# Expert gates in two halves, a reordered lead-in and earlier gathers in a two-layer metaformer kernel

## The reference, cut to what matters

```python
# layer 0 mixer, per image: depthwise 3x3 value and query; stride-2 key and offsets
o = gelu(ln(off) * ln_g + ln_b)                 # 28 x 28 points
offset = tanh(einsum(o, w_off2) + ref_points)   # sampling positions
sampled = bilinear(value, offset)               # 4 neighbours, gathered
x = x + w_out @ (query @ (key, sampled))        # linear attention
# both layers, per pixel t: mixture of experts
probs = softmax(ln(t) @ gate_w + gate_b)        # 4 experts
masked = probs * top2(probs); masked /= masked.sum() + 1e-9
t = t + sum_e masked[e] * (gelu(ln(t) @ w1[e] + b1[e]) @ w2[e] + b2[e])
# layer 1 mixer: sum of 7x7, 5x3, 3x5 and separable depthwise convolutions
```

## Time and profile before

| | |
|---|---|
| median of 3 runs | 1770.33 us (1766.41 to 1772.63) |
| the profiled execution: its time, its span | 1774.66 us, 1772.7 us |
| PE busy | 1429.3 us, 81% |
| DVE busy | 962.2 us, 54% |
| ACT busy | 681.6 us, 38% |
| POOL busy | 283.9 us, 16% |
| first matmul of slot 0 | at 300.4 us |
| steps 1 to 6 of slot 7 (nothing beside the experts) | 16.94 us each |

### The profile page before, as it was taken

One profiled execution on the slowest core, in us unless ns is written; L12 is line 12 of the kernel. 1 busy time (PEld: TensorE's weight loads), 2 busy tenths in 40 slices (PEclk: granted clock), 3 DMA queues, 4 the chain that ended last, 5 costly groups with the idle time before them and its releaser, 6 DMA issues.

```text
span 1772.7 us, 19232 instructions
## 1 busy us (share of the span) xinstructions
PE 1429.3 (81%) x6068; PEld 959.2 (54%) x6068; DVE 962.2 (54%) x2534; ACT 681.6 (38%) x1403; POOL 283.9 (16%) x189
## 2 busy tenths in 40 slices
PE   4120635888876999898976999899989999999898
PEld 2110324555544567665644567666766676666565
DVE  3968864747897454346887454444343443244323
ACT  3120023424543333344543334345344434355443
POOL 2514021701126000001117000000000000000000
PEclk9999955898997999999888999999999999999999
DMA  3441120413332322223323322234223412221121
GB/s 104 90 107 57 39 66 20 134 60 97 94 99 79 102 64 72 66 80 98 107 66 93 103 75 72 66 96 109 61 63 82 124 52 57 67 78 44 56 69 44
DMA packets 169510, 137.94 MB, mean 78 GB/s; under 512 B 114752, under 2 KB 163138, under 8 KB 169026
## 3 DMA queue, kind: packets, MB, share of 16 engines
q1 hardware_dynamic: 162802, 131.26, 27.2%
q0 software_dynamic: 3072, 4.82, 1.0%
q10 hardware_dynamic: 3536, 0.63, 0.2%
HBM read 97.02 MB, written 39.65 MB: 77 GB/s over the span
## 4 chain that ended last, share of the span: by engine, by line
issue 42%; PE 38%; POOL 10%; ACT 4%; DVE 3%; DMA 1%; ACTq 1%; SPq 1%; POOLq 0%; DVEq 0%
PE y_ps L898 15%; PE at_ps L1001 7%; POOL ln_rstd L811 5%; POOL pix_mem L824 5%; PE h_ps L906 4%; PE h_ps L907 4%; PE h_ps L905 4%; ACT ln_cen L679 2%; PE lg_ps L888 1%; PE lb_ps L879 1%; PE at_ps L954 1%; ACT hidden L772 1%; ACTq L655 1%; DVE vq_mem L1174 1%; DVE part L1130 0%
## 5 line engine op out<-in xcount | busy, mean ns | idle before, releaser
L772 ACT ACTIVATE hidden<-h_ps,b 128x448 f32<-128x448 f32 x672 | 425.0, 634 | 750.8 <-PE h_ps L907 746.6
L898 PE MATMUL y_ps<-hidden,w 128*96 128x448 f32 x1344 | 639.6, 560 | 44.6 <-ACT hidden L772 23.2
L905 PE MATMUL h_ps<-xh,w1h 96*128 96x448 f32 x672 | 476.2, 709 | 0.0
L1130 DVE SCALAR_TENSOR_TENSOR part<-y_ps,b,gate_t 96x448 f32<-96x448 f32 x224 | 151.8, 678 | 563.4 <-PE y_ps L898 511.2
L811 POOL TENSOR_TENSOR ln_rstd<-ln_ve,minus_half 112x4 f32<-112x4 f32 x112 | 161.2, 1439 | 1293.0 <-DVE ln_ve L1113 1292.8
L898 PEld LDWEIGHTS y_ps<-hidden,w 128*96 128x96 f32 x1344 | 207.9, 167 | 119.8 <-ACT hidden L772 58.0
L906 PE MATMUL h_ps<-xl,w1h 96*128 96x448 f32 x672 | 251.2, 374 | 0.0
L907 PE MATMUL h_ps<-xh,w1l 96*128 96x448 f32 x672 | 249.2, 371 | 0.0
L905 PEld LDWEIGHTS h_ps<-xh,w1h 96*128 96x128 f32 x672 | 131.1, 195 | 139.7 <-issue 124.7
L906 PEld LDWEIGHTS h_ps<-xl,w1h 96*128 96x128 f32 x672 | 132.1, 197 | 121.2 <-issue 120.4
L679 ACT ACTIVATE ln_cen<-ln_cen,ln_rstd 112x96 f32<-112x96 f32 x448 | 130.1, 363 | 149.0 <-POOL ln_rstd L811 148.9
(11 more groups left out here) (119 smaller groups left out, 1205.9 us busy)
## 6 DMA issues: line engine op xcount, KB each, us to landing
gate_t<-gates_dram SPq DMA_DIRECT2D x112, 336.0 KB
value_pairs<-pix_mem SPq DMA_DIRECT2D x56, 168.0 KB, 3.2
x_mem<-norm_c SPq DMA_DIRECT2D x16, 420.0 KB, 4.5
x_mem<-norm_a SPq DMA_DIRECT2D x16, 336.0 KB, 3.9
ln_x<-in_x SPq DMA_DIRECT2D x28, 168.0 KB
norm_a<-ln_cm SPq DMA_DIRECT2D x28, 168.0 KB, 2.0
res_mem<-in_x SPq DMA_DIRECT2D x4, 1176.0 KB, 9.6
x_attn<-res_mem SPq DMA_DIRECT2D x16, 294.0 KB, 2.7
```

The source lines that it names most:

```text
L772: act.activation(hidden[c % HID_RING][:, :], h_ps[c % H_BANKS][:, 0:TILE], ACT.Gelu, bias=b1[l][:, c:c + 1]).then_inc(gelu_done, 1)
L898: pe.matmul(y_ps[e % Y_BANKS][0:C, 0:TILE], w2[l][:, c, :], hidden[c % HID_RING][:, :], start=(j == 0), stop=(j == CPE - 1)).then_inc(hid_ ...
L905: pe.matmul(ps, hi, xh[:, ring(k)], start=True, stop=False)
L1130: dve.scalar_tensor_tensor(part[:, e, :], y_ps[e % Y_BANKS][0:C, 0:TILE], b2[l][:, e:e + 1], gate_t[e // 2][:, e % 2, :], ALU.add, ALU.mul ...
```

## The change

- Scores are read and gates made in two halves (tiles 0 to 3, then 4 to 6), each with its own buffers, in the last two steps before the slot; each half is turned and stored in the step after. SP asks for `gate_t` first thing in a slot and waits for the second half only at tile 4.
- In the lead-in DVE has its own order, with the late split behind the second job's statistics; the taps of stages 0, 2 and 3 are dealt otherwise, and in step L9 the first sampling stands before the taps. Image 1's stage 3 moves from L12 to L13.
- In every image `norm_off` goes to the end of stage 2, `apply_off` to the first place of stage 3, `offsets` and `positions` (with tanh) into stage 3.
- Images 0 and 1 turn their blocks through three banks (`at_ps` and both `y_ps`) and not one; image 0's final products too.
- Gathers: 2 in stage 3, then 4 and 4 in stage 4, 6 in stage 5. `scale_off` goes ahead of the place-0 scale_rows.
- `fold_taps` goes from behind L10 to behind slot 1 step 0, `load_taps` from slot 0 step 5 to slot 1 step 1.

```diff
-              11: [(1, 2)], 12: [(1, 3)]}
+              11: [(1, 2)], 13: [(1, 3)]}
-GATE_STEP = {(-1, LEAD - 1): 0, **{(slot, TILES - 1): slot + 1 for slot in range(SLOTS - 1)}}
+GATE_TILES = ((0, 4), (4, TILES))
+GATE_STEP = {(-1, LEAD - 2): (0, 0), (-1, LEAD - 1): (0, 1),
+             **{(slot, TILES - 2 + part): (slot + 1, part) for slot in range(SLOTS - 1) for part in range(2)}}
+GATE_TURN = {after: GATE_STEP[step] for step, after in zip(STEPS, STEPS[1:]) if step in GATE_STEP}
...
-        TURNS, KEY_TURNS = 2, 5
+        TURNS, KEY_TURNS = 3, 5
+        def spare(b, i):
+            return 2 if b == 0 or b == 1 and i < AT_KEY else 0
+        def at_bank(b, i):
+            return (at_ps, *y_ps)[i % 3] if spare(b, i) else at_ps
...
+                if i == 0 and m in (GATE_TILES[0][0], GATE_TILES[1][0]):
+                    sp.wait_ge(gates_st[u][m > 0], 16)
+                if u is not None and p == 0:
+                    load_gates(u, 0, 0)
+                    load_gates(u, 0, 1)
+                    load_res(u, 0)
                 if 6 in stages:
                     store_attn(stages[6], 0)
                 if 0 in coming:
                     load_norm(coming[0].n)
...
-                if u is not None and p == 0:
-                    sp.wait_ge(gates_st[u], 16)
-                    load_gates(u, 0, 0)
-                    load_gates(u, 0, 1)
-                    load_res(u, 0)
-                if (slot, p) == (0, 5):
+                if (slot, p) == (1, 1):
                     load_taps()
...
-                if stage == 3 and c == 7:
+                if stage == 3 and c == 5:
                     gelu_off(b)
-                if stage == 4 and c == 0:
+                if stage == 3 and c == 11:
                     tanh_pos(b)
-                    if (slot, p) in GATE_STEP and c == 10:
-                        exp_scores(GATE_STEP[slot, p])
+                    if (slot, p) in GATE_STEP and c == (8, 10)[GATE_STEP[slot, p][1]]:
+                        exp_scores(*GATE_STEP[slot, p])
...
-                if 0 in jobs:
-                    scale_rows(jobs[0])
                 if 3 in stages:
                     scale_off(stages[3])
+                if 0 in jobs:
+                    scale_rows(jobs[0])
                 if 4 in stages:
-                    gather(stages[4], 0, 5)
+                    gather(stages[4], 2, 6)
                 if 5 in stages:
                     gather(stages[5], 10, 2 * GQ)
                 if 1 in jobs:
                     scale_rows(jobs[1])
+                if 3 in stages:
+                    gather(stages[3], 0, 2)
                 if 4 in stages:
-                    gather(stages[4], 5, 10)
+                    gather(stages[4], 6, 10)
...
-                if m == 0 and u > 0:
-                    pe.wait_ge(g_scores_read, u)
+                if u > 0 and m == GATE_TILES[0][0]:
+                    pe.wait_ge(g_moved, 2 * u)
+                if m == GATE_TILES[1][0]:
+                    pe.wait_ge(g_scores_read, 2 * u + 1)
+                if m == GATE_TILES[1][0] + 1:
+                    pe.wait_ge(g_moved, 2 * u + 1)
...
+            ORDER_LEAD = ("normalize0", "combine0", "combine1", "normalize1", "split_late", "combine2", "split0", "scores",
+                          "combine3", "gates", "sum", "sum_experts", "sum_residual", "end")
-            TAPS_LEAD = {2: dict(none, normalize0=1, normalize1=1), 3: dict(none, combine1=1), 4: dict(none, combine1=1)}
-            BESIDE = {(2, "combine3"): norm_off, (3, "combine0"): apply_off, (3, "normalize1"): offsets,
-                      (4, "normalize0"): positions}
+            TAPS_LEAD = {0: dict(none, combine2=1, end=1), 2: dict(none, combine0=1, split_late=1),
+                         3: dict(none, combine0=2, end=3), 4: dict(none, combine1=1)}
+            BESIDE = {(2, "end"): norm_off, (3, "normalize0"): apply_off, (3, "combine1"): offsets,
+                      (3, "combine3"): positions}
-                        if name == "scores":
-                            read_scores(GATE_STEP[slot, p])
-                        if name == "gates":
-                            make_gates(GATE_STEP[slot, p])
+                        gates = GATE_STEP[slot, p]
+                        if name == ("normalize1", "scores")[gates[1]]:
+                            read_scores(*gates)
+                        if name == ("combine2", "gates")[gates[1]]:
+                            make_gates(*gates)
-                if (slot, p) == (-1, 10):
+                if (slot, p) == (1, 0):
                     fold_taps()
```

More of the change, by code:

```diff
@@ L226, in metaformer_kernel @@
         SE = E * SUBS
-        g_s = sb("g_s", [SUB, E, SUBS])
-        g_p = sb("g_p", [SUB, E, SUBS])
-        g_m = sb("g_m", [SUB, SUBS])
-        g_r = sb("g_r", [SUB, SUBS])
-        g_gt = sb("g_gt", [SUB, E, E, SUBS])
-        g_rank = sb("g_rank", [SUB, E, SUBS])
-        g_tr = sb("g_tr", [SE, SUB])
+        parts = [slice(first * NSUB, last * NSUB) for first, last in GATE_TILES]
+        subs = [some.stop - some.start for some in parts]
+        g_s = [sb(f"g_s{i}", [SUB, E, n]) for i, n in enumerate(subs)]
+        g_p = [sb(f"g_p{i}", [SUB, E, n]) for i, n in enumerate(subs)]
+        g_m = [sb(f"g_m{i}", [SUB, n]) for i, n in enumerate(subs)]
+        g_r = [sb(f"g_r{i}", [SUB, n]) for i, n in enumerate(subs)]
+        g_gt = [sb(f"g_gt{i}", [SUB, E, E, n]) for i, n in enumerate(subs)]
+        g_rank = [sb(f"g_rank{i}", [SUB, E, n]) for i, n in enumerate(subs)]
+        g_tr = [sb(f"g_tr{i}", [E * n, SUB]) for i, n in enumerate(subs)]
         x_mem = sb("x_mem", [128, CGROUPS * XCOLS])
@@ L333, in metaformer_kernel @@
         g_moved = sem("g_moved")
-        gates_st = [sem(f"gates_st{u}") for u in range(SLOTS)]
+        gates_st = [[sem(f"gates_st{u}_{i}") for i in range(2)] for u in range(SLOTS)]
         xq_ld = sem("xq_ld")
@@ L785, in _ @@
                         attention(b, stage, c)
-                    if (slot, p) in GATE_STEP and c == 10:
-                        exp_scores(GATE_STEP[slot, p])
-                    if p == 0 and c == 3 and u is not None:
-                        take_gates(u)
+                    if (slot, p) in GATE_STEP and c == (8, 10)[GATE_STEP[slot, p][1]]:
+                        exp_scores(*GATE_STEP[slot, p])
+                    if (slot, p) in GATE_TURN and c == 3:
+                        take_gates(*GATE_TURN[slot, p])
                 if (slot, p) == (-1, 2):
@@ L913, in turn @@
             def turn(b, i, src, width):
[L914 removed]
+                use(b, max(0, i - spare(b, i)))
                 for g in range(G):
[L916 removed]
+                    last = pe.transpose(at_bank(b, i)[0:width, g * 128:(g + 1) * 128], src(g), ident[:, :])
                 last.then_inc(at_full, 1)
@@ L943, in times_w_out @@
             def times_w_out(b, g):
-                use(b, AT_M2 + g)
-                pe.matmul(at_ps[:, 0:Q * C], kv[:, g, :], w_exp[:, g, :], start=True, stop=True)\
+                use(b, AT_M2 + max(0, g - spare(b, AT_M2)))
+                pe.matmul(at_bank(b, AT_M2 + g)[:, 0:Q * C], kv[:, g, :], w_exp[:, g, :], start=True, stop=True)\
                     .then_inc(at_full, 1)
@@ L951, in times_query @@
                 q, h = i // 2, i % 2
-                use(b, AT_Y + max(0, i - (b == 0)))
+                use(b, AT_Y + max(0, i - spare(b, AT_Y)))
                 for g in range(G):
-                    last = pe.matmul(y_bank(b, i)[0:C, 0:YCOL], m2[:, g, q * C:(q + 1) * C],
+                    last = pe.matmul(at_bank(b, AT_Y + i)[0:C, 0:YCOL], m2[:, g, q * C:(q + 1) * C],
                                      query[:, g, h * YCOL:(h + 1) * YCOL], start=(g == 0), stop=(g == G - 1))
@@ L1008, in _ @@
                 stages = attn_stages(slot, p)
+                if (slot, p) == (0, 0):
+                    pe.wait_ge(at_free, AT["attn", 1] + AT_KEY)
                 if u is not None:
@@ L1029, in _ @@
                         attention(b, stage, c)
-                    if p == 0 and c == 2 and u is not None:
-                        turn_gates(u)
+                    if (slot, p) in GATE_TURN and c == 2:
+                        turn_gates(*GATE_TURN[slot, p])
                     if (slot, p) in GEN_STEP and c in (3, 5, 7, 9):
@@ L1423, in _ @@
                         before = (TAPS_OF if slot >= 0 else TAPS_LEAD)[stage]
-                share = [before[name] if name in here else 0 for name in ORDER]
+                order = ORDER if slot >= 0 else ORDER_LEAD
+                share = [before[name] if name in here else 0 for name in order]
                 at = 0
-                for i, name in enumerate(ORDER):
+                for i, name in enumerate(order):
                     till = len(ops) * sum(share[:i + 1]) // sum(share)
```

112 lines of the change are left out of this document (56 added, 56 removed).

## The result

The changed kernel takes 1712.22 us (median of 4 runs, 1708.38 to 1717.21) against 1768.78 for the kernel before in the same comparison: ratio 0.968, 95% interval 0.9647 to 0.9713. The forecast was 1732 with a range from 1714 to 1754. The profiled execution took 1717.2 us, its span 1715.4.

A forecast was written before the change was run, and what follows sets the result against it. It took PE to bound the slots and a chain round the engines, mostly through DVE, the lead-in. Lead-in -25.0 and slots -13.5 gave -38.5 us: 1736.2 for the profile, 1731.8 for the median, range 1714 to 1754.

The forecast's parts named there:

- gate loads: First steps of slots 2 and 4 to 7: earlier loads on SP and shorter gates cut PE's wait, -9.5 us.
- step L4: Lead-in: both jobs' statistics go inside DVE's 6.00 us wait for x_mem, -3.5 us.
- L9's 3.0: Lead-in: image 1's first sampling goes ahead of the taps, inside DVE's 7.91 us wait for x_mem, -3.0 us.
- Step L6: Lead-in, turning image 0: three banks remove DVE's 6.17 us wait; of 6.70 some 5.2 stay; -7.7 us.
- Rival B: The lead-in gives half, as ACT's list becomes the bound where DVE was: 1745 us, chance 0.20.
- Steps L10 and L11: Lead-in: product additions wait less for PE, -3.5 us; the stretch to the third expert job's statistics shortens, -5.6 us.
- Steps L12 to L14: Lead-in's end, third expert job's statistics to slot 0: 60.7 us where 56.1 stood, +4.6 us.
- Second exponential: Slots 0 to 6: 1.6 us each in 1, 3 to 6, +8.0; with DVE's operations +3 each in 0 and 2, +6.
- Gathers and positions: Slots 0, 1, 3: gathers -6, +1 net with fold_taps, and -5 us; positions leaving step 0 of slots 1 and 3, -4.
- fold_taps: Leaves the lead-in, -6.3 us, and is paid again in slot 1, ahead of step 1's statistics.
- Rival C: The slots give nothing: second exponential at its upper bound (+6 more), fold_taps too (+6); 1744 us, chance 0.12.
- Rival D: Slower: PE's tile 4 scores in step 5 wait for DVE's first-half reading; 1777 at 6.5 us per slot, chance 0.09.

The follow-up runs named there:

- e2: Changed kernel with a slot's gates in one part again (one exponential, one store): 1711.32 us, 0.9640 of the kernel before.
- e4: Changed kernel with a slot's first gate loads back behind SP's other loads and stores: 1732.65 us, 0.9761 of the kernel before.
- e15: Changed kernel with the taps of stage 0 spread as before in the lead-in: 1729.44 us, 0.9736 of the kernel before.
- e16: e15 with the experts' constants issued in SP's list in step L7, not L4: 1727.54 us, 0.9751 of the kernel before.
- e14: Changed kernel with stage 3's lead-in taps in one group before the second combine, late split in its old place: 1716.96 us, 0.9675 of the kernel before.
- e12: Changed kernel with whole gates, fold_taps in slot 0 step 3, load_taps in slot 0 step 5, gathers 4, 4, 4, 4: 1695.85 us, 0.9567 of the kernel before.
- e7: Changed kernel with positions and tanh back in stage 4 and gathers in 5, 5 and 6: 1722.21 us, 0.9711 of the kernel before.
- e3: Changed kernel with fold_taps back in lead-in step 10 and its transfers in slot 0, step 5: 1713.28 us, 0.9653 of the kernel before.

## Why the prediction was right and wrong

The steps that failed are the term for the gate loads, with "Nothing is taken for the clock", and the 0 for slot 0's first tile: together -22.8 us where -9.5 stood. The lead-in gave 8.4 more than forecast, and the halves cost 6.1 less. The gathers alone erred the other way and gave 7.3 less. So the distance of some 19 us would be larger but for that.

*Gate loads.* The mechanism was right, the order of SP's list. The waiting came out as forecast, 10.0 us for 9.5, but partly by luck: the "1.2 by the shorter gates" did not carry (with whole gates the gain stays, e2), and in its place the loads landed sooner, 3.6 us from issue to `combine0` where 5.0 stood. What failed is the clock: 6.7 of the 16.7 us are PE at a higher granted clock. Of slot 5's 4.9 us, 2.5 are PE's wait and 2.4 the clock. And slot 0 was left out. Undoing the order costs its first tile 4.9 us (e4), as its loads too stood behind a store. With whole gates slot 0's first matmul comes 6.5 us earlier but its first tile only 0.5 (e2), so most of the 7 us that L13 was charged for the first half come back there.

*The lead-in, step L4.* "Both jobs' statistics stand ahead of all taps of stage 0, inside the wait: -3.5" is right as time on DVE. But with the statistics the tile's store moved too, and in SP's list behind it 15.7 us of constants and the next `in_x` load. The working priced DVE and left out SP. It also left out its own hazard: the power behind these statistics took 6.86 us with taps beside it and 1.27 without. Undoing the placement of stage 0's taps, for which the forecast had L4's 3.5 and L9's 3.0, costs 14.4 us (e15), of which SP's list accounts for 5.2 by `norm_off` (e16); another 3.5 have come by `norm_off`, as much as the forecast's term, and what makes up the 5.7 behind it, where L9's 3.0 stood, was not taken apart.

*Step L6* was right in its mechanism: the 6.17 are gone and 4.57 of 6.70 remain. It put all of its 7.7 us to the banks, though, and they are worth 4.5: with the banks undone and the order kept `norm_off` comes at 96.4, with the order undone and the banks kept at 99.7, with both at 91.9. So L4 was too small and L6 too large, and that their sum, -11.2 for -12.9, is so near is luck. Rival B (half of the lead-in) fell.

*Steps L10 and L11.* The 5.3 us of idle time fell to 0.4, where 3.5 had been taken; L11 gave 6.6 for 5.6. Right in kind, small in size. *Steps L12 to L14* were put at +4.6 with a wait of 4 us for GELU; in the trace the offsets follow the taps with no wait, and the steps cost +1.1. The terms as listed there add up to 61.6 us before the "two short waits", and not to 60.7, so the forecast's own +4.6 should have been over +5.5. The new place of the split, called worth nothing, was undone only together with the taps of stage 3 (e14: 3.0 for both).

*Second exponential.* Forecast +14 with the operations in slots 0 and 2, less 4; measured +3.9 over steps 5 and 6, of which 2.6 are a clock dip of that execution (last section). The 1.6 per exponential in slots 1, 3, 4 and 5 was 1.1, and step 6 was 1.2 us shorter in these slots and 0.9 in slot 6, 6 us in all where the second half had 4. In slots 0 and 2 the halves cost 0.9 us each (e2), not 3. The Trainium skill (ScalarE: Activation LUTs, "What ACT_TABLE_LOAD costs") has about 2.7 us for each switch with the drain, which the forecast turned into 5.3 more per slot; the traces disagree: 1.1 us of step per added exponential, and on ACT itself 2.9 us for two switches with the exponential between them (1301.95 to 1304.86 in slot 4 of the kernel before).

*Gathers and positions* gave half of what was forecast, 6.7 of 14. By slots: 0.0 for -6 in slot 0, -1.4 for -1 in slot 1, -5.4 for -7 in slot 3. The wait that was to shrink did not: DVE still waits 13.3 us in 3 places for the gathers, where 13.8 stood in the earlier trace rows. Everything before the sampling moved up, and the six gathers left for stage 5 were the limit again. "Two fewer take most of it" failed because the two fewer were in stage 4; e12, with two fewer in stage 5, took 11.5 of the 14.0 and 13 us of time. What slot 3 gained is mostly in PE's wait for the scaling behind the power, 6.7 us before and 2.0 after. In slot 0 the new places are worth 5.2 us in the changed kernel (e7), yet its step 1 is no shorter than in the kernel before; which other part of the change takes as much there was not tested.

*fold_taps* was right: -6.3 in the lead-in, paid again in slot 1 (e3: no change). Rival C did not come. Rival D's wait did, in small: PE is idle in step 5 for the first half's reading, by 2.3 us in slot 0 and 0.8 in slot 2, which the forecast had named as a sign of being wrong, but at 5.5 us per slot. The range had no bound for PE's clock, nor for what else stands in SP's list. Its upper end does not fit the rivals: B and C together give 1757, not 1754.

## What to carry to other kernels

When an operation is moved, follow what its result releases in every queue, the DMA-issuing one first: a store that goes out 15 us earlier takes everything behind it along, and that can be worth as much as the wait it was moved into. When a wait of the pacing engine goes, look at its busy time as well: here 6.7 of 16.7 us were the same work at a higher granted clock. Undo a change part by part, and try a part in the kernel before too: the constants' place was worth 5.2 us by `norm_off` in one kernel and 1.2 in the other. If a wait stays the same size after its work was moved up, look for the last piece left in the last stage, as the six gathers were.
